# Two phases joined into one block, and the transposes of the keys moved one tile later

## The chip, the cores and the metric

The kernel runs on one core of one Trainium2 chip. The metric is the device time of one execution in microseconds; the median of three runs is given. The core has five instruction streams, called engines here: PE (matmuls and transposes), DVE (vector), ACT (activation), POOL (GpSimd) and SP, which only issues DMAs.

## The reference

Two transformer layers on x of shape 8 x 256 x 512 (2,048 tokens of width 512), with a context of the same shape:

```python
x = x + L0_attention(layernorm(x), context)     # one head of 512
x = x + L0_ffn(layernorm(x))                    # ternary weights, 8-bit activations, hidden 2048
x = x + L1_attention(layernorm(x), context)     # 16 heads of 128, 4 key/value heads
x = x + L1_ffn(layernorm(x))                    # 8 experts, top 2, and a shared one
```

What the change touches is the making of keys and values of the second layer, the feed-forward part of the first layer, and the attention of the second:

```python
k = (context @ Wk + bk).reshape(b, se, 4, 128); v = (context @ Wv + bv).reshape(b, se, 4, 128)
k = k * rsqrt(mean(k * k, axis=-1) + 1e-6) * kn_w       # RMS norm of each head
...
q = rmsnorm((layernorm(x) @ Wq + bq)); out = softmax(q k^T / sqrt(128) + mask) v @ Wo
```

## The kernel before

The tokens are cut into T = 16 tiles of 128. Float32 products are made as three matmuls of split numbers (a high and a low part), in the helper `matmul3` (lines 78 to 80). The order of work is written by hand for each engine, with semaphores between them. The work is a row of phases, each a block with its own semaphores and its own buffers; between two phases stands a barrier of all engines (line 56), which no engine passes before all have done all that they have in the phase, the waits of SP for its DMAs among it. The phases, with the stretches of the profile in which they run:

- `attention0`, to about 308 us.
- `keys_values_ternary`, to about 450 us. For each tile t, PE makes `keys(t)` (12 matmuls) and `values(t)` (12 matmuls) in two banks each. DVE adds the bias (`biased`, line 742: bank to `kf`), ACT squares `kf` into `ksq` (`squares`, line 685), DVE sums the squares (line 746), ACT takes the root (line 689), DVE inverts it and multiplies it into `kf` itself (`normed`, line 752). PE transposes the four heads of the tile (`transposed`, line 838), and ACT writes the result to the staging buffer (`keys_out`, line 696), from which POOL stores two tiles at a time. PE's order in the loop is keys(t), transposed(t - 1), values(t). `biased(t)` waits until `transposed(t - 2)` has read `kf`. All of `kf`, `ksq` and the banks are double. Beside this, the three weight matrices of the feed-forward part are made ternary: their absolute sums on ACT in tiles 0 to 2, 6, 7, 11 and 12, then a sum over all (tiles 3, 8 and 13, with one small matmul, line 860, after values(t) on PE, and `scale_of`/`inverse_of` on DVE), and the rounding in tiles 4, 5, 9, 10, 14 and 15: four pieces a tile, scaled on ACT (line 705) and rounded on DVE (lines 777 and 779), one of them before `normed` and three after it.
- `ffn0`, to about 700 us. For each tile PE runs four quarters of the gate and value products (`up`), the transposes of the normalised input two tiles ahead, and `down(t - 2)`. SP moves the quantised hidden tile through a transposing DMA (`hqT`, line 943). The finished tile gets its sum (`add`, DVE line 1134), its statistics (lines 1139, 1143), the power -0.5 on POOL (`next_rstd`, line 977), the shift (line 1147), its norm on ACT (`next_norm`, line 1028), the transposes on PE (`next_xT`, line 1222), the high part on ACT (`next_hi`), the low part on DVE (`next_lo`), and two stores to DRAM on SP (lines 949 and 950). The loop runs to T + 5, so that the last tiles run out behind it. Once tile T - 3 is stored, SP loads the first two of the four chunks of 512 tokens of the normalised, transposed input (line 957) back from DRAM, 2 MB each (a high and a low megabyte), into buffers that lie over the gate and value weights.
- `attention1`, to about 1385 us. 64 units u (4 groups of heads, 4 chunks, 4 heads). It starts with `queries` of units 0, 1 and 2, `square_sums` (line 1581), `rstd` on POOL (line 1358), `scores`, `maxima` and `exp`, and goes on with a loop whose first PE instruction is `transposed(0)` (line 1608). Its first DMAs are small weights, 1.4 MB of expert weights, and keys and values of the next chunk.
- `feed_forward1`, to the end.

Of the kernel before, what the change touches and what calls it, by code (L numbers as in the profile page):

```python
# [539 lines left out]
def keys_values_ternary(nc, banks, X, eps, ones, ident, ahead, W, gamma, gb6, mv, rstd, f_dram, gb_dram, ctxT_dram, wv_dram,  # L540
# [12 lines left out]
    with Phase(nc) as ctx:  # L553
# [116 lines left out]
        def _(act):  # L670
# [44 lines left out]
            for t in range(T + 1):  # L715
# [8 lines left out]
                if t >= 1:  # L724
                    keys_out(t - 1)
# [6 lines left out]
                if t == T - 1:  # L732
                    act.wait_ge(s_mv, T)
                    act.activation(std[:], mv[:, :, 1], ACT.Sqrt, bias=eps[:]).then_inc(s_std, 1)

        @block.vector
        def _(dve):
            def biased(t):
                dve.wait_ge(s_k, t + 1)
                after(dve, s_kt, max(t - 1, 0))  # L740
# [7 lines left out]
            def normed(t):  # L748
# [3 lines left out]
                dve.tensor_tensor(kf[t % 2][:], kf[t % 2][:], rk[:, t, :].unsqueeze(2).broadcast_to([P, G, HD]),  # L752
# [72 lines left out]
        def _(pe):  # L825
# [23 lines left out]
            for t in range(T):  # L849
                keys(t)  # L850
                if t >= 1:
                    transposed(t - 1)
# [3 lines left out]
                if t in averaged:  # L856
# [7 lines left out]
def ffn0(nc, banks, X, eps, ident, W, gamma, gb6, mv, rstd, b_dram, x1T_dram, ahead, first, wq_dram, mask_dram, bq_dram,  # L864
         k_dram, v_dram, T):

    H = W[0].shape[2]
# [7 lines left out]
    C = first.K.hi.shape[1]  # L875
    wg, wv, wo = W
    group = lambda t: next(g for g, (a, b) in enumerate(GROUPS) if a <= t < b)
    with Phase(nc) as ctx:
        def sb(name, shape, dt=F32):
            return ctx.enter_context(nc.sbuf_tensor("f0_" + name, shape, dt))  # L880

# [3 lines left out]
        bv = sb("bv", [P, H])  # L885
        bo = sb("bo", [P, D])
        identb = sb("identb", [P, P], BF16)
        xn = sb("xn", [P, XS, D])
        xq = [sb(f"xq{j}", [P, D], BF16) for j in range(2)]
        xqT = [sb(f"xqT{j}", [P, KD, P], BF16) for j in range(3)]  # L890
        ax, qx, sx, sg, sv, rg = (sb(n, [P, T]) for n in ("ax", "qx", "sx", "sg", "sv", "rg"))
        r6 = sb("r6", [P, T, NR], BF16)
        rrest = sb("rrest", [P, T])
        rT = [sb(f"rT{j}", [P, P], BF16) for j in range(3)]
        gs = [sb(f"gs{j}", [P, 512]) for j in range(2)]
        vv = [sb(f"vv{j}", [P, 512]) for j in range(2)]
        h = [sb(f"h{j}", [P, H]) for j in range(2)]
        hq = sb("hq", [P, H], BF16)
        hqT = [sb(f"hqT{j}", [P, KH, P], BF16) for j in range(2)]
# [5 lines left out]
        x1n = [sb(f"x1n{j}", [P, D]) for j in range(2)]  # L905
        x1T = [Pair(ctx, nc, f"f0_x1T{j}", [P, KD, P]) for j in range(2)]
        gb, vb = banks[0:2], banks[2:4]
        x1b = banks[4]
        xb, ob = banks[6][:].bitcast(BF16), banks[7]
# [13 lines left out]
        s_chunk, s_raw, s_wqhi, s_wqlo = sem("next_chunks_loaded"), sem("next_loaded"), sem("next_w_hi"), sem("next_w_lo")  # L923
        s_hT, s_out, s_added = sem("hqT_transposed"), sem("out"), sem("added")

        ctx.start()
# [3 lines left out]
        def _(sp):  # L930
            sp.dma_start(bv[:], b_dram[1].partition_broadcast(P)).then_inc(s_b, 16)
# [6 lines left out]
            for n in range(T + 4):  # L938
                if n < T:
                    sp.wait_ge(s_hq, n + 1)  # L940
                    if n >= 2:
                        sp.wait_ge(s_out, n - 1)
                    sp.dma_start_transpose(hqT[n % 2][:], hq[:]).then_inc(s_hT, 16)
                t = n - 4
                if t < 0:
                    continue
                cols = slice(t * P, (t + 1) * P)
                sp.wait_ge(s_x1lo, t + 1)
                sp.dma_start(x1T_dram[0][:, :, cols], f32(x1T[t % 2].hi[:])).then_inc(s_x1st[t % 2], 16)
                sp.dma_start(x1T_dram[1][:, :, cols], f32(x1T[t % 2].lo[:])).then_inc(s_x1st[t % 2], 16)  # L950
                if t == T - 3:
                    sp.wait_ge(s_v, T * NH)
                    for j in range(2):
                        sp.wait_ge(s_x1st[j], 4 * 32)
                    for c in range(2):
                        for n, x in enumerate((first.xT[c].hi, first.xT[c].lo)):
                            sp.dma_start(f32(x[:]), x1T_dram[n][:, :, c * C:(c + 1) * C]).then_inc(s_chunk, 16)
            for j in range(2):
                sp.wait_ge(s_x1st[j], T // 2 * 32)
            sp.wait_ge(s_chunk, 64)  # L960

        @block.gpsimd
        def _(pool):
# [15 lines left out]
            for n in range(T + 3):  # L979
                for j in range(NH if n < T else 0):  # L980
# [8 lines left out]
                if n < T:  # L989
                    pool.wait_ge(s_xn, n + 1)  # L990
                    pool.tensor_tensor(X[:, n, :], X[:, n, :], bo[:], ALU.add).then_inc(s_bo, 1)
                if n >= 3:
                    next_rstd(n - 3)
                if n == 1:
                    for k, (pair, raw) in enumerate(first.splits):
                        pool.wait_ge(s_wqhi, k + 1)
                        pool.tensor_tensor(pair.lo[:], raw, f32(pair.hi[:]), ALU.subtract).then_inc(s_wqlo, 1)
# [1721 lines left out]
```

## Time and profile before

| | |
|---|---|
| median of 3 runs | 1899.9 us (1899.67 to 1900.98) |
| the profiled execution: its time, its span | 1900.31 us, 1898.6 us |
| PE, DVE, ACT, POOL busy | 92%, 65%, 45%, 30% of the span |
| mean granted clock of PE | 0.969 |

The span runs from the first to the last instruction; some 1.7 us of the execution's time lie around it. Busy shares are means over all phases. PE's clock is given as a share of its full 2.4 GHz: 0.5 is the lower of its two levels, 1.2 GHz.

### The profile page before, as it was taken

Reading aid. Unit: us, or ns where it says so; the run is one execution under the profiler, and the core shown is the slowest. Engines: PE = TensorE matmul, PEld = TensorE weight load, DVE = VectorE, ACT = ScalarE, POOL = GpSimd, SP = SyncE. Lnnn points to the kernel's source line nnn. Section 1 sums busy time; section 2 is a strip of 40 time slices with the busy share of each in tenths; the row PEclk is TensorE's granted clock in tenths of the full one; section 3 lists DMA queues with packets and bytes.
Section 4 is the critical chain, followed back from the end, with each engine's and each line's share of the span. In section 5 each row is a group of like instructions: output and inputs, shape, how many; then the busy total and the mean of one; then the engine's idle time right before and its main releaser. Section 6 shows DMA issues by size and latency. Waiting matters only on the chain. (4 is left out here: it accounts for less than half of the span.)

```text
span 1898.6 us, 26992 instructions
## 1 busy us (share of the span) xinstructions
PE 1756.0 (92%) x9951; PEld 1448.1 (76%) x9970; DVE 1238.1 (65%) x2357; ACT 852.2 (45%) x1621; POOL 560.1 (30%) x408
## 2 busy tenths in 40 slices
PE   6999996884799948999999999999888999999999
PEld 6989985672344428888888888888766789999876
DVE  4444434776898837766777766778756567676645
ACT  3322321774455525445555544555432255565411
POOL 2111111231666622121321212121120145464342
PEclk9999998997899978999999999999989999999999
DMA  6110114453133364121321212220042378888573
GB/s 221 34 33 22 33 44 145 159 201 117 33 67 79 89 189 136 56 79 57 123 83 62 78 56 79 64 98 6 1 170 112 108 258 274 285 283 267 195 245 106
DMA packets 160945, 225.38 MB, mean 119 GB/s; under 512 B 41654, under 2 KB 101302, under 8 KB 158646
## 3 DMA queue, kind: packets, MB, share of 16 engines
q1 hardware_dynamic: 150940, 189.50, 30.6%
q0 software_dynamic: 9888, 34.35, 5.8%
q8 instruction: 70, 1.15, 0.3%
q14 instruction: 47, 0.39, 0.1%
HBM read 171.65 MB, written 43.78 MB: 113 GB/s over the span
## 5 line engine op out<-in xcount | busy, mean ns | idle before, releaser
L1358 POOL TENSOR_TENSOR a_rq<-a_ssq,a_mhalf 128x4 f32<-128x4 f32 x64 | 65.2, 1018 | 414.5 <-DVE a_ssq L1482 414.5
L78 PE MATMUL bank<-a_xT_hi,a_wq_lo 128*128 128x512 f32 (+1 forms) x384 | 144.2, 375 | 18.8 <-PEq L56 15.8
L1443 ACT ACTIVATE a_pT_hi<-bank 128x512 fp32r<-128x512 f32 x128 | 69.6, 598 | 192.7 <-PE bank L1608 192.6
L1437 ACT ACTIVATE a_scores<-a_scores,a_nmax 128x256 f32<-128x256 f32 x256 | 127.2, 503 | 27.9 <-DVE a_nmax L1497 27.6
L79 PE MATMUL bank<-a_xT_lo,a_wq_hi 128*128 128x512 f32 (+1 forms) x384 | 138.7, 361 | 0.0
L80 PE MATMUL bank<-a_xT_hi,a_wq_hi 128*128 128x512 f32 (+1 forms) x384 | 138.5, 361 | 0.0
L78 PE MATMUL bank<-a_wo_hi,a_oT_lo 128*128 128x512 f32 x320 | 128.3, 401 | 2.8 <-DVE a_oT_lo L416 1.5
L80 PE MATMUL bank<-a_wo_hi,a_oT_hi 128*128 128x512 f32 x320 | 126.7, 396 | 0.0
L79 PE MATMUL bank<-a_wo_lo,a_oT_hi 128*128 128x512 f32 x320 | 126.5, 395 | 0.0
L1490 DVE SCALAR_TENSOR_TENSOR a_scores<-bank,a_rq,a_mask 128x256 f32<-128x256 f32 x256 | 106.1, 477 | 28.7 <-PE bank L80 20.4
L1897 POOL TENSOR_TENSOR e_wg_lo<-raw_g,e_wg_hi 128x1408 fp32r<-128x1408 f32 x26 | 91.4, 3514 | 112.9 <-ACT e_wg_hi L1964 112.9
L986 POOL TENSOR_TENSOR f_h<-f_vv,f_gs 128x512 f32<-128x512 f32 x64 | 95.6, 1495 | 85.0 <-DVE f_vv L1107 83.6
L78 PE MATMUL bank<-a_pT_hi,a_V_lo 128*128 128x256 f32 x384 | 109.6, 285 | 7.6 <-DVE a_pT_lo L1511 6.1
L1522 DVE TENSOR_TENSOR X<-X,bank 128x512 f32<-128x512 f32 x64 | 44.0, 688 | 105.0 <-PE bank L80 104.5
L80 PE MATMUL bank<-a_pT_hi,a_V_hi 128*128 128x256 f32 x384 | 108.8, 283 | 0.0
L79 PE MATMUL bank<-a_pT_lo,a_V_hi 128*128 128x256 f32 x384 | 108.6, 283 | 0.0
L78 PEld LDWEIGHTS bank<-a_xT_hi,a_wq_lo 128*128 128x128 f32 x384 | 74.2, 193 | 28.6 <-issue 19.6
L1511 DVE TENSOR_TENSOR a_pT_lo<-bank,a_pT_hi 128x512 fp32r<-128x512 f32 x128 | 82.1, 682 | 18.1 <-ACT a_pT_hi L1443 18.1
L1506 DVE TENSOR_SCALAR a_scores<-a_scores,a_rden 128x256 f32<-128x256 f32 x256 | 85.9, 398 | 2.3
L80 PEld LDWEIGHTS bank<-a_xT_hi,a_wq_hi 128*128 128x128 f32 x384 | 73.8, 192 | 11.3
L79 PEld LDWEIGHTS bank<-a_xT_lo,a_wq_hi 128*128 128x128 f32 x384 | 74.6, 194 | 8.9
L1497 DVE TENSOR_REDUCE a_nmax<-a_scores 128x2 f32<-128x512 f32 x128 | 81.2, 676 | 0.0
(404 smaller groups left out, 5344.1 us busy)
## 6 DMA issues: line engine op xcount, KB each, us to landing
raw_g<-in_egw SPq DMA_DIRECT2D x26, 704.0 KB, 8.6
raw_u<-in_euw SPq DMA_DIRECT2D x26, 704.0 KB, 10.5
a_xT_hi<-x1T_hi SPq DMA_DIRECT2D x16, 1024.0 KB, 6.0
a_xT_lo<-x1T_lo SPq DMA_DIRECT2D x16, 1024.0 KB, 8.2
raw_d<-in_edw SPq DMA_DIRECT2D x26, 512.0 KB, 4.0
y_routed<-m_y SPq DMA_DIRECT2D x39, 256.0 KB
raw_d<-in_edw SPq DMA_DIRECT2D x26, 192.0 KB, 4.3
a_cTraw<-in_ctxT SPq DMA_DIRECT2D x8, 512.0 KB, 3.5
```

Source lines behind the costliest of these rows:

```text
L78: pe.matmul(out, w[1], x[0], start=first, stop=False)
L79: pe.matmul(out, w[0], x[1], start=False, stop=False)
L80: return pe.matmul(out, w[0], x[0], start=False, stop=last)
L986: pool.tensor_tensor(h[n % 2][:, j * 512:(j + 1) * 512], vv[u % 2][:], gs[u % 2][:], ALU.mult).then_inc(s_h, 1)
L1358: pool.tensor_tensor(rq[:, h % HG, :], ssq[:, h % HG, :], mhalf[:], ALU.pow).then_inc(s_rq, 1)
L1437: act.activation(row, row, ACT.Exp, bias=nmax[:, i % 2, t:t + 1], accum_out=den[:, i % 2, t:t + 1]).then_inc(s_exp, 1)
L1443: act.activation(pT[b].hi[:], ptb[b][:].rearrange("p (k s) -> p k s", k=QT), ACT.Copy).then_inc(ft.hi, 1)
L1490: dve.scalar_tensor_tensor(sc[i % 2][:, r, :], scb[b][:, t * S:(t + 1) * S], rq[:, i % HG, r:r + 1], mask[:, t, :], ALU.mult, ALU.add).the ...
L1497: dve.tensor_reduce(nmax[:, i % 2, b * QT:(b + 1) * QT], sc[i % 2][:, b * QT:(b + 1) * QT, :], AX.X, ALU.max, negate=True).then_inc(s_nmax, 1)
L1506: dve.tensor_scalar(row, row, rden[:, i % 2, t:t + 1], None, ALU.mult).then_inc(s_p, 1)
L1511: dve.tensor_tensor(pT[b].lo[:], ptb[b][:].rearrange("p (k s) -> p k s", k=QT), f32(pT[b].hi[:]), ALU.subtract).then_inc(ft.lo, 1)
L1897: pool.tensor_tensor(pairs[w % 2].g.lo[:], raws[raw_of(w)].g[:], f32(pairs[w % 2].g.hi[:]), ALU.subtract).then_inc(s_glo, 1)
```

## The change

There are two parts.

In `keys_values_ternary` the transposes of a tile's keys stand one tile later in PE's order (keys(t), transposed(t - 2), values(t)), and so does ACT's `keys_out`. The normalised keys are written over the squares (`ksq`) and no longer over `kf`. `biased(t)` waits no more for transposes; `squares(t)` now waits for `transposed(t - 2)`, where it waited for the sum of squares of tile t - 2.

`ffn0` and `attention1` become one block, `ffn0_attention1`, with no barrier between them. The buffers of the attention lie over those of the feed-forward part by hand (`Region`), the bank of `next_xT` moves from 4 to 5, that of `down` from 7 to 6, that of the input transposes from 6 to 7. Waits on semaphores guard what was guarded by the barrier. What the last tiles of the feed-forward part leave to do after its 16 rounds is woven by hand into the start of the attention. SP loads chunk 0 before the transposing DMA of the last tile and chunk 1 behind it, in place of both after tile T - 3 was stored; POOL issues the load of Wo (1 MB) after its last product of the feed-forward part. The body of the 16 rounds and that of the attention's loop stay as they were.

```diff
             def squares(t):
                 act.wait_ge(s_kf, t + 1)
-                after(act, s_ksum, max(t - 1, 0))
+                after(act, s_kt, max(t - 1, 0))
...
-                if t >= 1:
-                    keys_out(t - 1)
+                if t >= 2:
+                    keys_out(t - 2)
...
+            keys_out(T - 1)
...
             def biased(t):
                 dve.wait_ge(s_k, t + 1)
-                after(dve, s_kt, max(t - 1, 0))
                 after(dve, s_ksq, max(t - 1, 0))
...
-                dve.tensor_tensor(kf[t % 2][:], kf[t % 2][:], rk[:, t, :].unsqueeze(2).broadcast_to([P, G, HD]),
+                dve.tensor_tensor(ksq[t % 2][:], kf[t % 2][:], rk[:, t, :].unsqueeze(2).broadcast_to([P, G, HD]),
...
-                    last = pe.transpose(ktb[t % 2][:, g * P:(g + 1) * P], kf[t % 2][:, g, :], ident[:])
+                    last = pe.transpose(ktb[t % 2][:, g * P:(g + 1) * P], ksq[t % 2][:, g, :], ident[:])
...
                 keys(t)
-                if t >= 1:
-                    transposed(t - 1)
+                if t >= 2:
+                    transposed(t - 2)
...
+            transposed(T - 2)
             transposed(T - 1)
```

The joined block, SP, with the stores and loads at the boundary:

```diff
-            for n in range(T + 4):
-                if n < T:
-                    sp.wait_ge(s_hq, n + 1)
...
-                if t == T - 3:
                     sp.wait_ge(s_v, T * NH)
                     for j in range(2):
-                        sp.wait_ge(s_x1st[j], 4 * 32)
-                    for c in range(2):
...
+                        sp.wait_ge(s_x1st[j], CT // 2 * 32)
+                    chunk(0)
+                hidden_transposed(t)
+                if t >= 4:
+                    next_stored(t - 4)
+            for j in range(2):
+                sp.wait_ge(s_x1st[j], CT * 32)
+            chunk(1)
+            sp.wait_ge(s_flo, len(first.splits))
+            keys_values(1)
+            for t in range(T - 4, T):
+                next_stored(t)
```

POOL, and what ACT and DVE have after the 16 rounds:

```diff
+            pool.wait_ge(s_flo, len(first.splits))
+            pool.dma_start(wraw[:], wo_dram[:, 0:HG, :]).then_inc(s_wload, 16)
+            for t in range(T - 3, T):
+                next_rstd(t)
+            rstd(0, 0)
+            rstd(1, 1)
...
+            round_h(T - 1)
+            next_hi(T - 5)
+            next_norm(T - 4)
+            queries(0, 0, 0, True)
+            next_hi(T - 4)
+            next_norm(T - 3)
+            queries(1, 0, 1, True)
+            next_hi(T - 3)
+            exp(0, 0)
+            next_norm(T - 2)
+            queries(2, 0, 2)
+            next_hi(T - 2)
+            next_norm(T - 1)
+            next_hi(T - 1)
...
+            ffn_add(T - 3)
+            quantised_h(T - 1)
+            next_stats(T - 3)
+            next_lo(T - 5)
+            next_mean(T - 3)
+            next_shift(T - 4)
+            ffn_add(T - 2)
+            next_stats(T - 2)
+            next_mean(T - 2)
             queries(0, 0)
+            next_lo(T - 4)
+            next_shift(T - 3)
             queries(1, 1)
+            ffn_add(T - 1)
+            next_stats(T - 1)
+            next_mean(T - 1)
             square_sums(0, 0)
             scores(0, 0)
             maxima(0, 0)
+            next_lo(T - 3)
+            next_shift(T - 2)
             queries(2, 2)
             square_sums(1, 1)
+            next_lo(T - 2)
+            next_shift(T - 1)
             scores(1, 1)
             maxima(1, 1)
+            next_lo(T - 1)
             normalise(0, 0)
```

PE, with the new waits of the first units and its order after the 16 rounds:

```diff
+                if begin:
+                    pe.wait_ge(s_gs, T * NH - 1 + u)
+                    pe.wait_ge(s_chunk[0], 32)
+                    pe.wait_ge(s_flo, len(first.splits))
...
             def transposed(u, n, i):
+                if u == 0:
+                    pe.wait_ge(s_x1lo, T)
...
+            next_xT(T - 5)
+            down(T - 2)
             queries(0, True)
+            next_xT(T - 4)
             queries(1, True)
+            down(T - 1)
             square_sums(0, 0)
+            next_xT(T - 3)
             scores(0)
             queries(2)
             square_sums(1, 1)
+            next_xT(T - 2)
             scores(1)
+            next_xT(T - 1)
```

ACT's `wo_hi(0)`, which writes over the buffers of `next_norm` and `next_hi`, waits until all 16 tiles are stored.

## Rows read from the trace of the kernel before

**Rows 1.** Stretches: length; busy PE, PEld, DVE, ACT, POOL; granted clock, DMA share, GB/s.

```profile
330.00:447.50 117.50, 97.09 (x432) 77.64 (x430) 89.03 (x171) 82.80 (x135) 26.59 (x28) 0.94 0.46 158
...
670.90:706.80 35.90, 10.72 (x53) 5.39 (x52) 10.73 (x24) 8.21 (x10) 3.86 (x9) 0.76 0.69 207
706.80:728.20 21.40, 16.43 (x84) 14.25 (x84) 8.52 (x20) 7.04 (x15) 3.09 (x5) 0.82 0.52 155
728.20:1385.00 656.80, 649.31 (x4008) 574.46 (x4009) 482.27 (x1092) 334.52 (x858) 140.65 (x106) 0.99 0.20 66
```

**Rows 2.** Waits, 325 to 452 us: us in total, times, longest.

```profile
PE bank L838 <- DVE kv_kf L752: 14.8, 6, 3.8
DVE kv_kf L742 <- PE bank L80: 9.3, 6, 2.6
```

**Rows 3.** Timeline of DVE, keys and values: start, length, what, idle before.

```profile
344.43 0.69 DVE L742 TENSOR_TENSOR kv_kf<-bank,kv_bk 128x512 f32<-128x512 f32 x1 [2.63 <-PE bank L80]
...
350.34 0.69 DVE L742 TENSOR_TENSOR kv_kf<-bank,kv_bk 128x512 f32<-128x512 f32 x1 [1.56 <-PE bank L80]
...
356.52 0.69 DVE L742 TENSOR_TENSOR kv_kf<-bank,kv_bk 128x512 f32<-128x512 f32 x1 [1.77 <-PE bank L80]
...
365.85 0.68 DVE L742 TENSOR_TENSOR kv_kf<-bank,kv_bk 128x512 f32<-128x512 f32 x1
...
392.93 0.69 DVE L742 TENSOR_TENSOR kv_kf<-bank,kv_bk 128x512 f32<-128x512 f32 x1 [1.09 <-PE bank L80]
```

**Rows 4.** Timeline of PE around the boundary.

```profile
673.35 3.61 PE L1244 MATMUL bank<-f_wo,f_hqT 128*128 128x512 bf16 x16 [1.83 <-DVE X L1134]
677.45 0.66 PE L1222 MATMUL bank<-ident,f_x1n 128*128 128x128 f32 x4 [0.49 <-ACT f_x1n L1028]
680.18 3.63 PE L1244 MATMUL bank<-f_wo,f_hqT 128*128 128x512 bf16 x16 [2.07 <-DMA f_hqT<-f_hq]
...
706.82 0.77 PE L78 MATMUL bank<-a_xT_hi,a_wq_lo 128*128 128x512 f32 x1 [15.78 <-PEq L56]
...
716.13 0.39 PE L78 MATMUL bank<-a_xT_hi,a_wq_lo 128*128 128x512 f32 x1
...
718.93 0.95 PE L1581 MATMUL bank<-ones,a_sq 128*128 128x1 f32 x8
...
728.24 1.97 PE L1608 MATMUL bank<-ident,a_scores 128*128 128x128 f32 x8 [2.52 <-DVE a_scores L1506]
```

**Rows 5.** Timeline of SP's queue around the boundary.

```profile
668.70 0.65 SPq L950 DMA_DIRECT2D x1T_lo<-f_x1T_lo  x1
675.85 1.64 SPq L943 DMA_TRANSPOSE f_hqT<-f_hq  x1
```

**Rows 6.** DMA view, 720 to 760 us: GB/s by slice; median us to landing.

```profile
GB/s 14 0 0 0 0 0 0 0 0 0 0 0 0 0 0 0 203 225 324 399 418 391 162 0 86 373 414 389 175 144 1 0 0 0 0 0 0 0 0 16
...
a_xT_hi<-x1T_hi SPq DMA_DIRECT2D x1, 1024.0 KB, 5.9
a_xT_lo<-x1T_lo SPq DMA_DIRECT2D x1, 1024.0 KB, 7.9
```

**Rows 7.** Timeline of DVE around the boundary.

```profile
683.85 0.75 DVE L1134 SCALAR_TENSOR_TENSOR X<-bank,f_so,X 128x512 f32<-128x512 f32 x1 [4.25 <-PE bank L1244]
...
717.38 1.66 DVE L1490 SCALAR_TENSOR_TENSOR a_scores<-bank,a_rq,a_mask 128x256 f32<-128x256 f32 x4 [1.26 <-POOL a_rq L1358]
```

**Rows 8.** Timeline of POOL around the boundary.

```profile
686.35 0.55 POOL L977 TENSOR_TENSOR f_rstd<-f_ve,f_mhalf 128x1 f32<-128x1 f32 x1
...
716.30 1.04 POOL L1358 TENSOR_TENSOR a_rq<-a_ssq,a_mhalf 128x4 f32<-128x4 f32 x1 [7.97 <-DVE a_ssq L1482]
```

**Rows 9.** Groups by line, 666 to 729 us: busy us, mean ns of one.

```profile
L1152 DVE TENSOR_TENSOR f_x1T_lo<-bank,f_x1T_hi 128x512 fp32r<-128x512 f32 x6 | 4.1, 686 | 5.2 <-ACT f_x1T_hi L1034 5.2
L1028 ACT ACTIVATE f_x1n<-X,f_nmr,f_rstd 128x512 f32<-128x512 f32 x5 | 4.1, 810 | 4.5 <-DVE f_nmr L1147 4.5
...
L1034 ACT ACTIVATE f_x1T_hi<-bank 128x512 fp32r<-128x512 f32 x5 | 3.0, 593 | 6.5 <-PE bank L1222 6.5
```

More of the change, by code:

```diff
@@ L860, in _, with ffn0_attention1 @@
                     pe.matmul(tot[:, w:w + 1], ones[:], asums[:, w:w + 1], start=True, stop=True).then_inc(s_tot, 1)
+            transposed(T - 2)
             transposed(T - 1)
-def ffn0(nc, banks, X, eps, ident, W, gamma, gb6, mv, rstd, b_dram, x1T_dram, ahead, first, wq_dram, mask_dram, bq_dram,
-         k_dram, v_dram, T):
+def ffn0_attention1(nc, banks, X, eps, ident, ones, area, limit, W, gamma, gb6, mv, rstd, b_dram, x1T_dram, ahead, first, wq1,
+                    wq_dram, wo_dram, mask_dram, bq_dram, k_dram, v_dram, last, last_drams, B, S, G):
+    T = B * S // P
     H = W[0].shape[2]
@@ L904, in ffn0 @@
         ve1, rstd1, nmr1 = (sb(n, [P, T]) for n in ("ve1", "rstd1", "nmr1"))
[L905 to L909, printed above, removed]
+        assert mem.offset <= limit
+        wq = [first.wq, wq1]
+        wraw, xT, mask, bq = ahead.raw, first.xT, first.mask, first.bq
+        gb, vb, x1b, fob, xb = banks[0:2], banks[2:4], banks[5], banks[6], banks[7][:].bitcast(BF16)
+        qb, scb, ptb, ob, ssb = banks[0:2], banks[2:4], banks[4:6], banks[6], banks[7]
         s_b, s_id = sem("biases_loaded"), sem("constants")
@@ L937, in _ @@
             sp.dma_start(first.Vraw, v_dram[:, 0:C // P, 0:P]).then_inc(s_raw, 16)
[L938 to L951 removed]
+            for t in range(T):
+                if t == T - 1:
@@ new lines, in keys_hi, with values_hi, queries @@
+            def keys_hi(n):
+                act.wait_ge(s_kraw, n * 16)
+                after(act, s_sc, (n - 1) * HG)
+                act.activation(K[n % 2].hi[:], first.Kraw, ACT.Copy).then_inc(s_khi, 1)
+            def values_hi(n):
+                act.wait_ge(s_vraw, n * 16)
+                after(act, fo.mm, (n - 1) * HG)
+                act.activation(V[n % 2].hi[:], first.Vraw, ACT.Copy).then_inc(s_vhi, 1)
+            def queries(u, g, i, begin=False):
+                act.wait_ge(fq.mm, u + 1)
+                if not begin:
+                    act.wait_ge(s_ssq, u - 1)
+                if g:
+                    act.wait_ge(s_bqg, g)
+                b = bqg[g % 2][:, i % HG:i % HG + 1]
+                act.activation(sq[i % 2][:], qb[i % 2][:], ACT.Square, bias=b).then_inc(s_sq, 1)
+                act.activation(q[i % 2].hi[:], qb[i % 2][:], ACT.Identity, bias=b).then_inc(fq.hi, 1)
@@ new lines, in exp, with transposed @@
+            def exp(u, i):
+                for t in range(CT):
+                    act.wait_ge(s_nmax, u * NB + t // QT + 1)
+                    row = sc[i % 2][:, t, :]
+                    act.activation(row, row, ACT.Exp, bias=nmax[:, i % 2, t:t + 1],
+                                   accum_out=den[:, i % 2, t:t + 1]).then_inc(s_exp, 1)
+            def transposed(u):
+                for b in range(NB):
+                    act.wait_ge(ft.mm, u * NB + b + 1)
+                    act.activation(pT[b].hi[:], ptb[b][:].rearrange("p (k s) -> p k s", k=QT), ACT.Copy).then_inc(ft.hi, 1)
@@ L1036, in _, with output @@
+            def output(u, n, i):
+                act.wait_ge(fo.mm, u + 1)
+                if i % HG == 0:
+                    after(act, s_out, n * CT)
+                act.activation(oT.hi[:, i % HG, :], ob[:], ACT.Copy).then_inc(fo.hi, 1)
             act.wait_ge(s_id, 6)
```

615 lines of the change are left out of this document (284 added, 331 removed).

## The prediction

> **What bounds the kernel now.** I first read busy time by stretch [rows 1], then who waits for whom where keys and values are made [rows 2] and the order of time there [rows 3], then the four queues around the boundary of the two phases to be joined [rows 4, 5, 7, 8]. PE bounds the whole, but not everywhere. In the attention of the second layer it is busy for 649.3 of 656.8 us: nothing can be won there but by starting sooner. Two stretches are different. Where keys and values are made PE is busy for 97.1 of 117.5 us, DVE for 89.0, ACT for 82.8, and the busy times of DVE and ACT hide that they hand each tile to and fro. Around the boundary PE is busy for 10.7 us of 35.9, at a granted clock of 0.76, and then for 16.4 of 21.4 us at 0.82 while the attention fills up [rows 1]. The change is aimed at these two. The sum is made in the profiled execution's time (1900.31 us, of which the span is 1898.6); the median shown is 0.4 us less.
>
> **Part one: the transposes one tile later.** What it removes is PE's wait for the normalised keys at line 838, 14.8 us in 6 waits [rows 2]. That is the most that could be won here, and I don't count it, since PE isn't late with respect to its own work but to DVE's. What counts is where DVE waits for PE: at line 742, the bias of a new tile, 9.3 us in 6 waits [rows 2]. Everything on DVE follows that instruction, and the phase ends with DVE (its last rounding, the last values and their store). So the gain is what of these six waits goes.
>
> - Tiles 2, 3 and 4 start at 344.43, 350.34 and 356.52, after waits of 2.63, 1.56 and 1.77 us [rows 3]. After the change PE goes from keys(1) straight to values(1) and keys(2), 3.2 us sooner, so keys(2) are ready before DVE wants them and the 2.63 go whole. With PE then a product ahead the 1.56 of tile 3 go too, but for some 0.1. Tile 4 stands behind the small matmul of the averages (line 860), which PE meets before keys(4): the sum of squares of tile 3 must be there, then 12 matmuls of keys(4) follow, which take 2.8 us at full clock, as from 716.13 to 718.93 [rows 4]. Of the 1.77 us about 0.9 go. Together 5.0 us.
> - Tiles 4 and 5, 9 and 10, 14 and 15 are rounded. From 356.52 to 365.85 one of them takes 9.33 us with no wait for PE in it [rows 3]; PE's own work for a tile is two products of 2.8 us and the transposes, 6.2 us. Here the loop of DVE and ACT sets the pace before and after, and PE's waits only change their place: from line 838 to the wait for a free bank. Nothing is won.
> - Tile 9 starts at 392.93 after 1.09 us [rows 3], again behind the averages' matmul, which keeps its place: nothing. Two further waits, together 9.3 - 2.63 - 1.56 - 1.77 - 1.09 = 2.2 us, are at tiles 13 and 14, where ACT's absolute sums and the averages come last: nothing, or 0.3.
>
> What it adds is one wait: ACT's squares(t) stand behind the transposes of tile t - 2, which PE runs right after keys(t). Four transposes take 0.66 us [rows 4], and the bias that squares(t) waits for anyway takes 0.69 us from the same moment [rows 3]: covered. Without that cover (PE at half clock) it would be some 0.5 us a tile, behind squares(t) being ACT's root and its weight pieces, for which DVE waits. ACT has one `keys_out` more at the end, while DVE still rounds: covered. Bounds of part one: nothing at the one end, 9.3 us at the other; I take 5.0, with the rest of DVE's waits left as they are.
>
> **Part two: the joined block.** I follow the tail and the start as one chain and ask when PE can run `transposed(0)` of the attention, which was at 728.24 [rows 4]; from there on the loop is as before.
>
> 1. When does PE find its first queries? SP is free at 668.70 + 0.65 = 669.35 [rows 5], the value products are done by then, and chunk 0 goes out there instead of at 687. Its two loads land 5.9 and 7.9 us after issue where nothing else moves [rows 6]; the second is issued some 0.6 us later: 669.35 + 0.6 + 7.9 = 677.9. PE comes from down(14) at 673.35 + 3.61 = 677.0 [rows 4]. So the queries start at 678.
> 2. PE's order is then queries(0) 2.8, four transposes 0.66, queries(1) 2.8, down(15) 3.6 [rows 4]: 678 + 9.9 = 687.9. The transposed hidden tile for down(15) was issued by SP at 675.85 [rows 5] and used at 680.18 [rows 4]; it is wanted only at 684.3 now, so its wait of 2.07 us is gone, and it may come 4 us later than it did. In the kernel before down(15) ended near 683.8: it moves back by 4 us, and that costs nothing but what hangs on it.
> 3. What hangs on it is the first scores. POOL has the power of tile 15 ahead of rstd(0). From the sum on DVE to the end of that power it was 683.85 to 686.90, 3.05 us [rows 7, 8]; then the power of unit 0 with 1.04 us [rows 8]. From 687.9 + 0.2 that makes 692.2, against 717.38 before [rows 7].
> 4. From the first scores to `transposed(0)` it was 728.24 - 717.38 = 10.9 us [rows 4, 7], of which one wait of 2.5 is on DVE. Woven into this now are, on ACT, two norms of 0.81 and two high parts of 0.59, and three low parts of 0.69 on DVE [rows 9]. Only those of tiles 14 and 15 are in the chain, since `transposed(0)` waits for the low part of tile 15; I follow exp(0), norm(14), queries(2), high part(14), low part and shift, norm(15), transposes, high part(15), low part(15) and come to 12.2 us, 1.3 more. That makes 704.4.
> 5. For what can't be read from the rows I add 2.0 us: POOL's 1 MB of Wo now goes out at about 673 beside chunk 0, and some of the first 24 matmuls may run at half clock, as the first ones at 706.82 did (0.77 us against 0.39) [rows 4]. This gives 706.4, and a gain of 728.2 - 706.4 = 21.8 us.
>
> The Trainium skill (DMA: Bandwidth & Descriptors, Where 436 GB/s comes from) says that between DRAM and a core's memory about 358 GB/s is the limit. Taken as an estimate, the 3 MB of chunk 0 and Wo would need 8.8 us from 669.35 on and a latency besides, and the sum would come out some 2 us later than step 1, which the allowance of step 5 would just hold. The slices of the trace show 414 and 418 GB/s for moments [rows 6], so the measurement is above that limit, and the sum stays with the landing times.
>
> Bounds of part two: at most all of PE's idle time from 670.9 to 728.2, 25.2 + 5.0 = 30.2 us [rows 1]; at least the wait at the barrier alone, 15.78 us [rows 4], if filling costs what it did and the tail's 4 us of step 2 come on top: 12.
>
> Sum: 5.0 + 21.8 = 26.8; 1900.3 - 26.8 = 1873.5 in the profiled execution's terms, 1873 for the median.
>
> **The rivals.**
>
> - *The keys' part gives nothing.* DVE and ACT lose as much to the new wait and to the limits of their own loop as the three waits give. For it: both are near their limit on 13 of 16 tiles. Against it: the waits of tiles 2 to 4 are plain. 1899.9 - 21.8 = 1878. Chance 0.13.
> - *All of PE's waits there are won.* The phase shortens by 14.8 us: it would need rounded tiles below 9.3 us, which no row supports. 1863. Chance 0.05.
> - *The tail stays in the way.* Work is woven in order on ACT and DVE; if chunk 0 comes late (SP, Wo) or the one chain of step 4 is longer by all its pieces, each late piece holds those behind it, and half of what lies between 21.8 and 12 is kept: a gain of 12 to 16 and 5. 1881. Chance 0.20.
> - *The attention's loop pays for it.* Its buffers and banks lie elsewhere now, and weights and chunks are loaded in another order beside it. The stretch from 728.20 has 64 units of 10.3 us [rows 1]. If each lost 0.42 us the gain of 26.8 would be gone, and from 0.48 us the kernel is slower: at 1 us a unit 1937. Nothing in the profile speaks for it: the loads are the same ones, and DMA is at a share of 0.20. Chance 0.02 slower, 0.02 about even.
>
> **How the numbers follow.** The forecast as summed has 0.58, and its own range is 1868 to 1878 (0 to 9.3 around the 5.0, and 2 to 3 us around step 5). The range over the cases reaches from 1864 to 1883: it leaves out about 0.15. Faster by over 0.2% (3.8 us, about what a measurement of this kernel tells from no change) is every case but the last: 0.96; the same 0.02, slower 0.02.
>
> **What would show it.** In the new trace, PE has no wait at the keys' transposes except for the last tile, DVE's bias of tile 4 starts about 5 us sooner, and rounded tiles still take 9.3 us. At the boundary PE runs queries 7 to 9 us after the last products of the rounds; the first scores on DVE come about 25 us sooner and `transposed(0)` about 22 us sooner relative to the end of the rounds; the loop from there to the end takes the same time. The prediction is wrong if a DMA (chunk 0, or the hidden tile behind it) is what PE waits for at down(15), if rounded tiles change their length, or if the loop does.

## The result, and the profile after

The changed kernel takes **1874.7 us** (median of 4 runs, 1873.6 to 1876.0) against 1900.2 us (4 runs, 1899.7 to 1901.0) for the kernel before: a ratio of **0.9866, 95% interval 0.9848 to 0.9883**. 1873 was forecast. The profiled span is 1872.9 us against 1898.6. That the total came out right hides errors of opposite sign, and the rows below show them.

**Where keys and values are made.** Waits of the kernel after, 325 to 452 us (total, times, longest), to be held against [rows 2]:

```profile
DVE kv_kf L742 <- PE bank L80: 7.4, 3, 3.7
PE bank L860 <- DVE kv_asums L764: 6.7, 3, 3.8
PE bank L78 <- DVE kv_vst L760: 4.1, 2, 2.2
PE bank L838 <- DVE kv_ksq L752: 3.3, 1, 3.3
```

PE's wait at the keys' transposes has shrunk from 14.8 to 3.3 us and is left at the last tile alone. But DVE still waits 7.4 us for PE, and the averages' matmul (line 860) now has 6.7 us of waiting ahead of it. DVE's timeline in the kernel after, for [rows 3] (tiles 0, 4, 5, 8, 9, 13, 14 and 15):

```profile
333.39 0.67 DVE L742 TENSOR_TENSOR kv_kf<-bank,kv_bk 128x512 f32<-128x512 f32 x1
...
353.23 0.69 DVE L742 TENSOR_TENSOR kv_kf<-bank,kv_bk 128x512 f32<-128x512 f32 x1 [1.09 <-PE bank L80]
...
362.56 0.68 DVE L742 TENSOR_TENSOR kv_kf<-bank,kv_bk 128x512 f32<-128x512 f32 x1
...
382.43 0.67 DVE L742 TENSOR_TENSOR kv_kf<-bank,kv_bk 128x512 f32<-128x512 f32 x1
...
392.28 0.69 DVE L742 TENSOR_TENSOR kv_kf<-bank,kv_bk 128x512 f32<-128x512 f32 x1 [3.75 <-PE bank L80]
...
421.52 0.67 DVE L742 TENSOR_TENSOR kv_kf<-bank,kv_bk 128x512 f32<-128x512 f32 x1
...
430.23 0.69 DVE L742 TENSOR_TENSOR kv_kf<-bank,kv_bk 128x512 f32<-128x512 f32 x1 [2.61 <-PE bank L80]
438.63 0.68 DVE L742 TENSOR_TENSOR kv_kf<-bank,kv_bk 128x512 f32<-128x512 f32 x1
```

In what follows a tile's start is counted from that of tile 0. Tile 4 starts at 19.84, where it was 24.81 (356.52 less 331.71, tile 0's start in the trace of before): 4.97 us won. Tile 5 comes 9.33 us behind tile 4, as before. Tile 9 starts at 58.89 (61.22 before): only 2.3 left. Tile 15 starts at 105.24 (106.11 before): 0.9 left. PE's timeline shows what happened ahead of tile 9:

```profile
382.12 0.39 PE L80 MATMUL bank<-kv_wv_hi,kv_cT_hi 128*128 128x512 f32 x1
386.33 0.59 PE L860 MATMUL bank<-kv_asums,ones 128*128 128x1 f32 x2 [3.83 <-DVE kv_asums L764]
386.78 0.77 PE L78 MATMUL bank<-kv_wk_hi,kv_cT_lo 128*128 128x512 f32 x1
387.35 0.63 PE L79 MATMUL bank<-kv_wk_lo,kv_cT_hi 128*128 128x512 f32 x1
387.78 0.63 PE L80 MATMUL bank<-kv_wk_hi,kv_cT_hi 128*128 128x512 f32 x1
```

In the kernel before, the same small matmul had a pause of 1.17 us ahead of it:

```profile
389.63 0.38 PE L860 MATMUL bank<-kv_asums,ones 128*128 128x1 f32 x2 [1.17 <-DVE kv_asums L764]
```

The stretches give the granted clock (the number before the last two), first of the kernel after, then of the kernel before, each with the 12 matmuls of keys(9) in it:

```profile
386.30:392.30 6.00, 5.97 (x16) 4.71 (x17) 1.88 (x7) 1.33 (x3) 1.27 (x1) 0.50 0.59 196
```

```profile
389.60:392.90 3.30, 3.27 (x16) 2.71 (x17) 1.86 (x6) 1.34 (x3) 1.28 (x1) 1.00 0.58 200
```

PE is ahead of DVE now, so it stands 3.83 us at the averages' matmul, whose sums DVE has yet to make. Behind that pause keys(9) run at the lower of the two clocks (0.50, 1.2 GHz), a matmul every 0.43 us where it was 0.23, and DVE waits 3.75 us for them.

**At the join.** PE's timeline of the kernel after, for [rows 4]:

```profile
667.93 3.62 PE L1556 MATMUL bank<-f_wo,f_hqT 128*128 128x512 bf16 x15
671.39 0.60 PE L1534 MATMUL bank<-ident,f_x1n 128*128 128x128 f32 x4
673.82 3.61 PE L1556 MATMUL bank<-f_wo,f_hqT 128*128 128x512 bf16 x16 [1.83 <-DVE X L1347]
681.48 0.47 PE L78 MATMUL bank<-a_xT_hi,a_wq_lo 128*128 128x512 f32 x1 [4.05 <-issue]
...
689.38 3.40 PE L1556 MATMUL bank<-f_wo,f_hqT 128*128 128x512 bf16 x15
...
708.69 1.73 PE L1615 MATMUL bank<-ident,a_scores 128*128 128x128 f32 x7 [2.18 <-DVE a_scores L1399]
```

SP's queue and the first scores on DVE, for [rows 5, 7]:

```profile
669.22 0.61 SPq L981 DMA_DIRECT2D a_xT_hi<-x1T_hi  x1
669.87 0.66 SPq L981 DMA_DIRECT2D a_xT_lo<-x1T_lo  x1
676.32 5.45 SPq L987 DMA_TRANSPOSE f_hqT<-f_hq  x1
```

```profile
696.44 1.66 DVE L1383 SCALAR_TENSOR_TENSOR a_scores<-bank,a_rq,a_mask 128x256 f32<-128x256 f32 x4 [1.88 <-POOL a_rq L1066]
```

The wait of 15.78 us at the barrier is gone. From the start of down(13) to `transposed(0)` it was 728.24 - 667.47 = 60.8 us and is 708.69 - 667.93 = 40.8: 20.0 won, 21.8 forecast.

**The rest.** Nothing was forecast for the attention's loop. From `transposed(0)` to the next phase's first matmul it took 660.7 us and takes 657.0. Its projection (Wo) is the product whose mean moved most; groups of PE, 740 to 1350 us, after and then before:

```profile
L78 PE MATMUL bank<-a_wo_hi,a_oT_lo 128*128 128x512 f32 x240 | 95.2, 397 | 1.5
L79 PE MATMUL bank<-a_wo_lo,a_oT_hi 128*128 128x512 f32 x240 | 93.6, 390 | 0.0
L80 PE MATMUL bank<-a_wo_hi,a_oT_hi 128*128 128x512 f32 x240 | 93.4, 389 | 0.0
```

```profile
L78 PE MATMUL bank<-a_wo_hi,a_oT_lo 128*128 128x512 f32 x240 | 96.4, 402 | 1.2
L80 PE MATMUL bank<-a_wo_hi,a_oT_hi 128*128 128x512 f32 x240 | 94.9, 396 | 0.0
L79 PE MATMUL bank<-a_wo_lo,a_oT_hi 128*128 128x512 f32 x240 | 94.8, 395 | 0.0
```

That is 402 + 396 + 395 - 397 - 390 - 389 = 17 ns for each of 256 threes, 4.4 us. The product of the attention's weights and the values went the other way, from 284, 281 and 281 ns to 286, 284 and 284, about 2 us over as many threes. The span's account: start of tile 0 later by 1.7 (ahead of every edit, so one execution against another), keys' phase -0.9, from there to down(13) -0.4, join -20.0, loop -3.7, last phase -2.4 (its code is the same; in the traces of the runs below it takes 506.6 to 508.4 us, and 509.7 in this one of before, so that is chance). Sum -25.7.

### The profile page after: what moved, and what is told of

Its sections match the earlier page's. It is cut to its first block and busy times, and to the rows that moved or that the text cites. A ratio compares the mean times of both kernels' runs of the same rounds, so it can differ in the third digit from the quotient of the medians.

```text
span 1872.9 us, 26972 instructions
## 1 busy us (share of the span) xinstructions
PE 1750.7 (93%) x9950; PEld 1448.0 (77%) x9970; DVE 1237.3 (66%) x2357; ACT 851.5 (45%) x1621; POOL 559.4 (30%) x408
## 5 line engine op out<-in xcount | busy, mean ns | idle before, releaser
L1066 POOL TENSOR_TENSOR a_rq<-a_ssq,a_qhalf 128x4 f32<-128x4 f32 x64 | 65.1, 1018 | 404.2 <-DVE a_ssq L1375 404.2
L79 PE MATMUL bank<-a_xT_lo,a_wq_hi 128*128 128x512 f32 (+1 forms) x384 | 138.5, 361 | 0.0
L79 PE MATMUL bank<-a_wo_lo,a_oT_hi 128*128 128x512 f32 x320 | 125.3, 392 | 0.0
L79 PE MATMUL bank<-a_pT_lo,a_V_hi 128*128 128x256 f32 x384 | 109.4, 285 | 0.0
L78 PEld LDWEIGHTS bank<-a_xT_hi,a_wq_lo 128*128 128x128 f32 x384 | 74.0, 193 | 16.9 <-issue 8.0
L78 PEld LDWEIGHTS bank<-a_pT_hi,a_V_lo 128*128 128x128 f32 x384 | 74.1, 193 | 9.7 <-DVE a_oT_lo L1409 6.8
L79 PEld LDWEIGHTS bank<-a_xT_lo,a_wq_hi 128*128 128x128 f32 x384 | 74.7, 194 | 8.9
```

The costliest lines, as they stand in the source:

```text
L78: pe.matmul(out, w[1], x[0], start=first, stop=False)
L79: pe.matmul(out, w[0], x[1], start=False, stop=False)
L1066: pool.tensor_tensor(rq[:, h % HG, :], ssq[:, h % HG, :], qhalf[:], ALU.pow).then_inc(s_rq, 1)
```

## Experiments

Each was timed beside the kernel before on the same chip; ratios are to that kernel, with their 95% intervals, and are the safer comparison between two of these kernels. "Tile 15" is its start on DVE behind tile 0, "join" is the start of down(13) to `transposed(0)`, "loop" from there to the next phase, all from the profiled execution.

### The two parts, each alone

e1_join_only has the joined block, and the old keys and values. e2_keys_only is the reverse. The edit that e1 takes back and e2 has alone:

```
-                after(act, s_ksum, max(t - 1, 0))
+                after(act, s_kt, max(t - 1, 0))
...
-                after(dve, s_kt, max(t - 1, 0))
...
-                dve.tensor_tensor(kf[t % 2][:], kf[t % 2][:], rk...
+                dve.tensor_tensor(ksq[t % 2][:], kf[t % 2][:], rk...
...
-                if t >= 1:
-                    transposed(t - 1)
+                if t >= 2:
+                    transposed(t - 2)
```

> The joined block with the keys' part as it was before. Theory (the keys' part is worth 0.9 us, since the 5.0 us won by tile 4 are lost again in two products at half clock): 1875.5 us. Rival (the keys' part is worth the 5.0 us of the forecast, and the trace of after shows an accident of one execution): 1879.7 us.

> The keys' part alone, two phases with the barrier. Theory: within 1.5 us of the kernel before, about 1899.3 us; DVE's bias of tile 4 about 5 us sooner in its phase, and the last one of tile 15 at most 1 us sooner. Rival: 1895 us, with the bias of tile 15 also 5 us sooner.

Measured: e1 **0.9865 (0.9846 to 0.9883)**, 1871.5 us; e2 **0.9993 (0.9983 to 1.0004)**, 1898.0 us. The join has all of the gain, and the keys' part gives nothing that can be measured. In e2's trace tile 4 starts at 19.82 (the 5 us are there) and tile 15 at 105.36. In e1 it is 24.85 and 106.07.

### Is it the pause, or PE's work?

e5_filled gives PE more to do: 12 matmuls whose result nobody reads, into a free bank, ahead of the averages' matmul of tiles 8 and 13.

```
                     w = averaged[t]
+                    for k in range(4 if w else 0):
+                        matmul3(pe, banks[7][:], part(wk, slice(None), k, slice(0, P)), part(wk, slice(None), k), True, True)
                     pe.wait_ge(s_asum, w + 1)
```

> The changed kernel with 12 matmuls of 128x512 that nobody reads, put on PE before the averages' matmul of tiles 8 and 13, where PE waited for 3.83 and 2.20 us. Theory (the gap before that matmul halves PE's clock, and the keys' product behind it, for which DVE waits, then takes 5.3 us in place of 2.9): the bias of tile 9 comes some 7.2 us after that of tile 8 in place of 9.85, though PE has more to do, and from tile 12 to tile 14 it takes some 14 us or less; 3 us less than the changed kernel in all, 1871.7 us. Rival (the product is late for its own reasons, another wait or the order): no change or 0.6 us more, 1874.7 to 1875.3 us.

Measured: **0.9850 (0.9836 to 0.9863)**, 1870.5 us. Timeline of PE and DVE in e5_filled where [rows 3] and the rows above have tile 9, and a stretch with its clock:

```profile
386.23 0.38 PE L862 MATMUL bank<-kv_asums,ones 128*128 128x1 f32 x2 [1.07 <-DVE kv_asums L764]
386.47 0.48 PE L78 MATMUL bank<-kv_wk_hi,kv_cT_lo 128*128 128x512 f32 x1
386.78 0.40 PE L79 MATMUL bank<-kv_wk_lo,kv_cT_hi 128*128 128x512 f32 x1
```

```profile
389.52 0.69 DVE L742 TENSOR_TENSOR kv_kf<-bank,kv_bk 128x512 f32<-128x512 f32 x1 [1.08 <-PE bank L80]
```

```profile
386.00:389.00 3.00, 2.77 (x13) 2.35 (x14) 2.03 (x8) 1.39 (x3) 1.28 (x1) 1.00 0.70 244
```

The averages' matmul stands where it stood (52.97 us behind tile 0, and 52.94 in the kernel after), and only the pause ahead of it is filled. Keys(9) run at full clock, tile 9 starts at 56.26 and tile 15 at 101.25, 4.0 us sooner than in the kernel after.

One trace isn't enough here, since how deep the clock cuts differs between executions: over the six traces with the same keys' code and the averages in place (after, e2, e3, e7, e8, e12) tile 15 starts at 102.6 to 105.4. All six in a table: the pause ahead of the averages' matmul, the mean granted clock from it to DVE's bias of the next tile, and DVE's wait there, in us.

| trace | tile 9: pause, clock, DVE's wait | tile 14: pause, clock, DVE's wait |
|---|---|---|
| before | 1.17, 1.00, 1.09 | none, 1.00, 1.19 |
| after | 3.83, 0.50, 3.75 | 2.20, 0.65, 2.61 |
| e2 | 3.83, 0.65, 2.68 | 3.83, 0.50, 3.75 |
| e3 | 2.22, 1.00, 1.08 | 3.84, 0.50, 3.75 |
| e7 | 2.21, 0.65, 2.52 | 2.22, 0.65, 2.67 |
| e8 | 2.21, 1.00, 1.07 | 3.85, 0.65, 2.68 |
| e12 | 2.24, 0.67, 2.42 | 2.24, 0.65, 2.60 |
| e5 (filled) | 1.07, 1.00, 1.08 | none, 1.00, 1.28 |

DVE's wait goes with the clock: 1.1 to 1.3 us at 1.00, 2.4 to 2.7 at 0.65 to 0.67, 3.75 at 0.50. The length of the pause alone doesn't give the clock (2.2 us stands beside 1.00 twice and beside 0.65 to 0.67 five times), but with the pause filled there was no low clock at either tile, and tile 15 came sooner than in all six. So it is the clock behind the pause, not PE's work, that held DVE. With the clock at 1.00 in both places tile 15 starts 106.11 - 101.25 = 4.9 us sooner than in the kernel before: the 5.0 that part one was forecast to give. The kernel's time alone doesn't show this, as the intervals of e5 and after overlap.

e6_average_later takes the averages' matmul out of the way instead: behind the next tile's keys and transposes, ahead of its values.

```
-                values(t)
-                if t in averaged:
-                    w = averaged[t]
+                if t - 1 in averaged:
+                    w = averaged[t - 1]
                     pe.wait_ge(s_asum, w + 1)
                     ...
+                values(t)
```

> The changed kernel with the averages' matmul of tiles 3, 8 and 13 one product later, behind the keys of the next tile, so that no product that DVE waits for stands behind it. Theory: DVE's three waits for PE (1.09, 3.75 and 2.61 us) go, the bias of tile 15 comes 98 to 99 us after that of tile 0 (105.2 in the changed kernel, 106.1 before), and the kernel takes 1867.5 us. Rival (ACT and DVE are the limit there anyway, so the waits only change their name): 1873 to 1875 us and 104 to 105 us.

Measured: **0.9833 (0.9820 to 0.9846)**, 1866.5 us. DVE no longer waits for PE at line 742 at all; tile 15 starts at 98.78, 7.3 us sooner than with the old order. Waits of PE in e6_average_later, 325 to 452 us:

```profile
PE bank L78 <- DVE kv_vst L760: 6.1, 3, 3.1
PE bank L838 <- DVE kv_ksq L752: 5.4, 1, 5.4
...
PE bank L859 <- DVE kv_asums L764: 0.7, 1, 0.7
```

e11_averages_later_in_old_order makes the same move in e1, where the transposes stand in their old place.

```
                 if t >= 1:
                     transposed(t - 1)
...
-                if t in averaged:
+                if t - 1 in averaged:
...
+                values(t)
```

> The joined block, with the keys' part of the change undone (transposes in the next tile's turn, normalised keys in place), and the averages' matmul behind the next tile's keys and transposes. If the keys' part is worth its forecast 5 us once the averages' matmul is out of PE's way, this takes some 5 to 7 us more than the kernel after with the same move (1866.5): 1871.5 to 1873, with DVE's bias of tile 4 at 24.8 and of tile 15 some 103 to 105 us behind tile 0. If the move alone does it and the keys' part is worth nothing at all, it takes 1866 to 1867, tile 15 at 99 to 100.

Measured: **0.9870 (0.9855 to 0.9885)**, 1874.0 us, tile 15 at 106.49. The four kernels together:

| | averages' matmul in place | averages' matmul later |
|---|---|---|
| old order of the transposes | e1: 0.9865 | e11: 0.9870 |
| transposes one tile later | after: 0.9866 | e6: 0.9833 |

Each edit alone is worth nothing that can be measured; both together are worth 0.0032 of 1899, 6.1 us. In the old order PE stands at line 838 anyway (16.9 us in 6 waits in e11), so the small matmul delays next to nothing (tile 9 starts at 60.99 in e11 and 61.21 in e1); with the new order it was the one thing left that held keys(t) to DVE's pace.

### What holds the first queries

e7_wo_load_later puts POOL's load of Wo behind the power of unit 0.

```
-            pool.dma_start(wraw[:], wo_dram[:, 0:HG, :]).then_inc(s_wload, 16)
...
             rstd(0, 0)
+            pool.dma_start(wraw[:], wo_dram[:, 0:HG, :]).then_inc(s_wload, 16)
```

> The changed kernel with POOL's load of Wo (1 MB) issued behind the first power of the attention and no longer beside chunk 0. Theory (chunk 0 is late because Wo shares the DMA engines with it): PE's first queries 2 to 3 us sooner behind down(14) (7.7 us in the changed kernel), transposed(0) as much sooner, 1872.3 us. Rival (the 2 MB themselves and their latency set it): below 1 us. If Wo then comes late for the first split of it, ACT waits there and the gain is given back at once.

Measured: **0.9848 (0.9834 to 0.9861)**, 1869.8 us. POOL's and PE's timelines in e7_wo_load_later:

```profile
689.60 0.87 POOL L1115 DMA_DIRECT2D ahead_raw<-in_Wo  x1
```

```profile
671.20 3.61 PE L1556 MATMUL bank<-f_wo,f_hqT 128*128 128x512 bf16 x16 [1.83 <-DVE X L1347]
676.30 0.48 PE L78 MATMUL bank<-a_xT_hi,a_wq_lo 128*128 128x512 f32 x1 [1.49 <-issue]
```

PE's pause ahead of the first queries is 1.49 us, and 1.41 in e10 with the same move. In the seven traces that have Wo's load beside chunk 0 and the chunk in its place (after, e1, e3, e5, e6, e11, e12) it is 2.06 to 4.05, 3.2 on average; the one of after is the longest. The join takes 37.3 and 36.9 us with the load later, and 37.2 to 41.4, 39.5 on average, without. So by the traces the load is worth some 2 us, where the one pair of e7 and after says 3.4; the ratios differ by 0.0018, 3.4 us, and their intervals overlap. The pause shows the load's effect clear of its spread, the kernel's time doesn't.

e8_chunk0_behind issues chunk 0 behind the last transposing DMA of the hidden tiles in place of ahead of it.

```
-                    chunk(0)
                 hidden_transposed(t)
+                if t == T - 1:
+                    chunk(0)
```

> The changed kernel with chunk 0 loaded behind the transposing DMA of the last tile and no longer ahead of it. Theory (the first queries wait for chunk 0, and everything of the start hangs on them in PE's order): queries and transposed(0) 6 to 8 us later, 1881.5 us. Rival (the tail of tile 15 sets the start of the attention, whatever the queries do): below 2 us, 1875 to 1876.5 us.

Measured: **0.9904 (0.9889 to 0.9919)**, 1880.5 us. Timelines of SP and PE in e8_chunk0_behind:

```profile
675.18 2.16 SPq L987 DMA_TRANSPOSE f_hqT<-f_hq  x1
677.39 0.59 SPq L981 DMA_DIRECT2D a_xT_hi<-x1T_hi  x1
```

```profile
687.50 0.76 PE L78 MATMUL bank<-a_xT_hi,a_wq_lo 128*128 128x512 f32 x1 [11.34 <-issue]
```

The transposing DMA's issue takes 2.16 us here and 5.45 in the kernel after, behind chunk 0, where nobody waited for it. The chunk goes out 4.8 us behind down(14)'s start in place of 4.6 us ahead of it, the queries start 14.9 us behind it in place of 7.7, and the kernel takes 5.8 us more by the medians and 7.2 by the ratios, whose intervals don't overlap. So the first queries hang on the chunk: its place ahead of the transposing DMA is worth 6 to 7 us, and most of the join's gain doesn't hang on it.

### The projection's matmuls

All of these change nothing but where buffers lie. In bytes from the start of a partition, the kernel before has Wo at 142816 and oT at 196096, the kernel after has 196096 and 167424.

e3_wo_32_off is the kernel after with Wo 32 bytes further and of the large buffers nothing else moved. The others are less clean: e4_before_wo_aligned is the kernel before with Wo and all of the attention's buffers behind it 32 bytes further, e9_before_both_aligned has another gap behind Wo, so that those behind it lie 64 bytes further, and e12_oT_32_off is the kernel after with oT 32 bytes further and pT, V and Wo, which lie behind it, 64 bytes further. The text recorded ahead of e12 says "Wo where it was"; its edit moves it.

```
+        over.offset += 32
         wo = over.pair("a1_wo", [P, HG, D])
```

```
+        sb("gap", [P, 8])
         wq, wo = [first.wq, wq1], pair("wo", [P, HG, D])
+        sb("gap_behind", [P, 8])
```

```
+        over.offset += 32
         oT = over.pair("a1_oT", [P, HG, C])
+        over.offset += 32
         pT = [over.pair(f"a1_pT{b}", [P, QT, S]) for b in range(NB)]
```

> The changed kernel with the buffer of Wo 32 bytes further on, so that it starts at 32 above a multiple of 64 bytes, as it did in the kernel before; nothing else moves but the small buffers behind it. Theory (the projection's matmuls are some 5 ns cheaper each in the changed kernel because of where Wo lies): 768 of them, 3.8 us more, 1878.5 us, and spacings of the projection's matmuls of 0.234 us in place of 0.227. Rival (they are cheaper for another reason, such as the neighbours' traffic): 1874.7 us and spacings as they are.

> The kernel before with 32 bytes left free ahead of the attention's buffers, so that Wo starts at a multiple of 64 bytes (the others behind it move by 32 too). Theory of the place of Wo: 3.8 us less than the kernel before, 1896.4 us, and spacings of 0.227 us in the projection. Rival: 1900.2 us. If buffers whose start is now no multiple of 64 bytes cost as much, the time does not fall and the spacings of the other matmuls rise.

> The kernel before with 32 bytes left free ahead of Wo's parts and 32 behind them, so that both operands of the projection's matmuls (oT and Wo) start at a multiple of 64 bytes; in the run with one gap Wo started at such a multiple and oT had lost it, and nothing was won. Theory (both operands have to be aligned): the projection's matmuls follow each other every 0.227 us in place of 0.234 to 0.235, the loop from transposed(0) to feed_forward1 takes some 656.5 us in place of 660.7 to 661.8, and the kernel takes 1894 to 1895 against 1899 (ratio 0.9975 to 0.998). Rival (the gain of the loop belongs to the joined block, by the order of its loads or what lies beside Wo): spacing and time as in the kernel before, ratio 0.9995 to 1.0005.

> The kernel after with oT 32 bytes further, Wo where it was: the mirror of the run in which Wo lay 32 bytes further. If either operand off a multiple of 64 costs, the projection's matmuls follow each other every 0.234 us in place of 0.227, the loop from transposed(0) takes 661 to 662 us, and the kernel 5 us more than the kernel after: 1879 to 1880, ratio 0.989 to 0.990. If only Wo (the moving operand) counts, it takes as long as the kernel after, 0.9866, spacing 0.227.

| kernel | Wo, oT: start modulo 128 | L79, mean ns | loop, us | ratio |
|---|---|---|---|---|
| before | 96, 0 | 395 | 660.7 | 1 |
| after | 0, 0 | 390 | 657.0 | 0.9866 |
| e3 | 32, 0 | 395 | 662.1 | 0.9877 (0.9860 to 0.9893) |
| e4 | 0, 32 | 396 | 661.8 | 0.9995 (0.9986 to 1.0004) |
| e9 | 0, 64 | 395 | 660.7 | 0.9997 (0.9986 to 1.0009) |
| e12 | 64, 32 | 395 | 659.6 | 0.9886 (0.9870 to 0.9901) |

In the eight traces with 0, 0 (after, e1, e5 to e8, e10, e11) the loop takes 656.2 to 658.3 us; in the five others of the table and in e2 it takes 659.6 to 662.1. One row each, groups of PE, 740 to 1350 us, of e3_wo_32_off, e9_before_both_aligned and e12_oT_32_off:

```profile
L79 PE MATMUL bank<-a_wo_lo,a_oT_hi 128*128 128x512 f32 x236 | 93.3, 395 | 0.0
```

```profile
L79 PE MATMUL bank<-a_wo_lo,a_oT_hi 128*128 128x512 f32 x240 | 94.7, 395 | 0.0
```

```profile
L79 PE MATMUL bank<-a_wo_lo,a_oT_hi 128*128 128x512 f32 x235 | 92.8, 395 | 0.0
```

That the place is the cause is shown by e3: 32 bytes take the 5 ns of each matmul back, with the same instructions and the other large buffers where they were. In the kernel's time that isn't clear of noise (0.9877 and 0.9866, intervals overlapping). e12 agrees, but it moved Wo too, so it doesn't show that oT alone would do it. Its loop is shorter than e3's by 2.5 us, most of which is the product of pT and V, which with both of these 64 bytes further takes 281 to 284 ns in place of e3's 284 to 287. My rule for the place fell twice: Wo at a multiple of 64 (e4), and both at multiples of 64 (e9), brought nothing. What remains possible is 128, or that both start at the same place within 128. For the second speaks the first layer's product of keys and queries, with both operands at 96: in the trace of before 389 and 391 ns for the second and third of its three matmuls, against 397 and 396 for its values' product with operands at 32 and 96. The queries of this layer speak for it only in part: with their input at 32 they take 394 ns where Wq lies at 0 and 392 where it lies at 32. No run moved Wo and oT together to another common place, so this stays open.

### The better version

e10_both_moved is the kernel after with the moves of e6 and e7.

> The kernel after with both of the moves that won alone: the averages' matmul behind the next tile's keys, and Wo's load behind the power of unit 0. They lie in different phases, so if each keeps its own gain (8.2 and 4.8 us of the medians) it takes 1874.7 - 13.0 = 1861.7 us, ratio 0.980 to 0.981. By the traces the first alone is worth about 6.5 us (tile 15 at 98.8 in place of 105.2) and the second 3.4 (down(13) to transposed(0) 37.3 in place of 40.8), together 9.9: 1864.8, ratio 0.982. The rival is that PE's sequence at the boundary is set by something else once it comes sooner (the powers on POOL, the stores of the tail), which gives no more than the first move alone, 1866.5.

Measured: **0.9815 (0.9802 to 0.9828)**, 1863.0 us, 36 below the kernel before beside it. Against the kernel after that is 9.7 us by the ratios (11.7 by the medians, which weren't taken beside each other). Tile 15 starts at 98.70, and the join takes 36.9 us: both keep their gain.

## Why the prediction was right in total, and where it was not

**Part one** (5.0 us forecast; e2 measured 0.0007 of 1899, 1.3 us, from a loss of 0.8 to a gain of 3.2).

- Tiles 2 to 4: right. 4.97 us won at tile 4.
- Rounded tiles keep 9.33 us: right, 353.23 to 362.56.
- What tile 4's averages' matmul waits for was misnamed: it is the sum over all of the absolute sums (DVE line 764), not the sum of squares of tile 3. It cost the sum little: 0.7 us went (a wait of 1.77 became 1.09) where 0.9 was taken.
- The step that failed is the third, "Tile 9 starts at 392.93 after 1.09 us, again behind the averages' matmul, which keeps its place: nothing", and with it the sentence on tiles 13 and 14, "nothing, or 0.3". They were costed as if PE came to that matmul as before. Measured against the moment when its sums are ready PE comes 2.7 us sooner, its pause grows from 1.17 to 3.83 us (2.2 in other executions), and the product behind the pause, the one that DVE waits for, runs in part or whole at half clock. DVE waits 3.75 us there for 1.09, and 2.61 at tile 14 for 1.19. e5 and e6 show both halves of it: with the pause filled the phase is 4.9 us shorter than before, as forecast, and with the matmul out of the way 7.3. The rival "the keys' part gives nothing" had the result with another cause: neither the new wait nor the limits of ACT's and DVE's own loop had a part in it, since in e5 and e6, with both, the gain is there.

**Part two** (21.8 forecast; 20.0 in the profile; the four traces with the barrier, before, e2, e4 and e9, have 60.4 to 60.8, 60.5 on average, and the seven traces above 39.5, which makes 21.0).

- Step 1, the queries' start at 678: 681.48, with this execution 0.5 late, so 3 us late. Wo's load is some 2 of them (e7). The allowance of 2.0 in step 5 was made for this and for half clock; it pays for 2.0 of the 3.8 us that steps 1 to 3 came late, and the other 1.8 are the difference of 21.8 and 20.0.
- Step 2: down(15) found its hidden tile ready, as said, though the transposing DMA's issue took 5.45 us (1.64 before). It ends at 692.8 for 687.9: step 1's delay, and 1.4 us more, with half clock in part of the first queries (from 683.0 to 685.5 the granted clock is 0.50, and a matmul shows 0.63 us for 0.39).
- Step 3: from the end of down(15) to the scores 3.7 us, 4.3 forecast. The scores are at 696.44 for 692.2.
- Step 4: 12.2 us forecast from the scores to `transposed(0)`, 708.69 - 696.44 = 12.25 measured. The rival "the tail stays in the way" didn't come.
- "From there on the loop is as before" was wrong by 3.7 us, in the kernel's favour: the projection's rows moved, by where Wo came to lie. The prediction itself named a changed loop as a sign of being wrong. Another of its signs was off as well: counted from down(13), the first scores came 21.4 us sooner, where about 25 was forecast.

So the total was right by luck. Of 5.0 forecast only 0.9 came in the profiled pair, and of 21.8 only 20.0. Against these 5.9 stand 3.7 of the loop, which weren't forecast, and 2.4 of the last phase, which are chance. The join's mechanism was right on its own. In the prediction the limit of 358 GB/s of the Trainium skill (DMA: Bandwidth & Descriptors, Where 436 GB/s comes from) put chunk 0 some 2 us later than my sum did. The trace of after agrees with a delay of that size (3.0 us, Wo's load in it), though not with the rate as a ceiling; data rate by slice, 660 to 700 us:

```profile
GB/s 0 0 0 16 0 0 0 173 290 330 274 223 125 256 406 401 420 367 270 398 288 164 290 323 279 178 176 268 397 399 406 331 301 342 249 80 0 0 0 0
```

It reaches 420 in a slice, above that limit, and falls to 125 between: here the peak of a slice was no measure of when 3 MB had landed.

## What to carry to other kernels

When an engine is let run ahead, look for the next thing in its order that still waits for the old pace, however small: here a matmul of one column. Move it in the same edit, because each edit alone measured as nothing and both as 6 us. And when a block is laid out anew in memory, compare the mean time of each product before and after: 32 bytes decided over 5 us of the loop's trace, and the gain would have been booked to the join.

## What the hardware did that I had not expected

- With 12 matmuls more at each of two places the keys' phase was 4.0 us shorter than in the trace of after (1.4 to 4.1 over the six traces), and the kernel 3 (ratio 0.9850 for 0.9866, with intervals that overlap), since the granted clock stayed at 1.00 where it had been 0.50 behind a pause of 3.83 us. Behind pauses of 2.2 us it was 1.00 in two places and 0.65 to 0.67 in five.
- The time of a 128x512 matmul in the projection is 390 or 395 ns by where Wo starts, with no other large buffer moved (e3): 5 us over 768 of them (loop 657.0, and 662.1 with Wo 32 bytes further).
- The issue of one transposing DMA took 4.8 to 5.5 us in the seven traces where chunk 0 (2 MB, the same queue) went out ahead of it and Wo's load (1 MB, POOL's queue) beside it. Behind chunk 0 but with Wo's load later it took 2.36 and 2.28 (e7, e10), with Wo's load beside it but the chunk behind 2.16 (e8), and 1.64 before [rows 5]. So it was neither the queue nor Wo alone.
